# A two-layer attention and expert kernel: its loop of steps replaced by a written-out order for the whole run

## The reference

```
x += attention(ctx, layernorm(x), mask)         # 8 heads of 16, 77 keys, softmax over masked logits
x += ffn(layernorm(x))                          # [x,-x] -> 512 -> 512 -> 128, weights +1/-1 from booleans, relu*2
x += (rmsnorm(layernorm(x)) * g_res) @ W_in.T + b_in + depool(rmsnorm(ctx)[:128], marks)
x += sum of the top 2 of 8 experts, by softmax gate, each with x @ W.T + b
# depool: bidx = cumsum(lens) - 1; boundary_mask.at[bidx].set(1); plug = clip(cumsum(boundary_mask) - 1, 0, 76);
# out row = scan(decay)[plug]; here as a product with pick[k, s] = (plug >= k) * exp(-DT * distance)
```

## Time and profile before

| | us |
|---|---|
| median of 3 runs | 601.62 (600.94 to 605.16) |
| profiled execution, its own time | 600.24 |
| its span | 598.4 |
| TensorE busy / VectorE / ScalarE / POOL | 504.2 / 451.4 / 345.6 / 364.9 |
| mean granted clock of TensorE | 0.958 |
| `a_exponent`, one of its two instructions | 1.105 |
| `rs` of an `rstd` on POOL, L399 | 1.022 |
| `out_x` store, issue to landing | 2.7 |

### The profile page before, as it was taken

The page is one execution under the profiler, slowest core; times in us unless marked ns, Lnnn a source line. Parts: engine busy times, 40 slices in busy tenths (PEclk is TensorE's granted clock), DMA queues, the critical chain, the costliest instruction groups (busy, mean ns, idle before and its releaser), DMA issues.

```text
span 598.4 us, 15067 instructions
## 1 busy us (share of the span) xinstructions
PE 504.2 (84%) x5467; PEld 322.6 (54%) x5467; DVE 451.4 (75%) x1501; ACT 345.6 (58%) x737; POOL 364.9 (61%) x630
## 2 busy tenths in 40 slices
PE   0374298999999999999999999999899999896763
PEld 0263156667565656565665656565757565552320
DVE  4499566888888888888889797979797978865342
ACT  1245267897767676666667676667676666333100
POOL 3103122464858686776868686959595858778457
PEclk9997589999999999999999999999999999999678
DMA  3600001101020202020101101020200000000000
GB/s 77 162 2 1 13 2 46 46 3 46 2 64 1 64 1 63 3 63 2 48 18 35 31 8 57 2 64 2 64 1 25 1 26 2 18 19 1 18 19 18
DMA packets 28578, 16.92 MB, mean 28 GB/s; under 512 B 3828, under 2 KB 28505, under 8 KB 28505
## 3 DMA queue, kind: packets, MB, share of 16 engines
q1 hardware_dynamic: 28504, 15.96, 9.4%
HBM read 11.71 MB, written 4.21 MB: 27 GB/s over the span
## 4 chain that ended last, share of the span: by engine, by line
PE 40%; DVE 22%; POOL 19%; DMA 8%; issue 7%; SPq 2%; ACT 1%; POOLq 0%; DVEq 0%; ACTq 0%
PE pc L1238 14%; DMA cx<-in_ctx 7%; PE pa L1104 5%; PE pb L1140 5%; PE pb L1147 4%; POOL sum L453 4%; DVE st L585 4%; DVE marks L569 3%; POOL rs L399 3%; POOL sum L455 2%; PE pa L1115 2%; PE pb L1159 2%; DVE mx L610 2%; DVE h L690 2%; DVE weighed L780 2%
## 5 line engine op out<-in xcount | busy, mean ns | idle before, releaser
L1238 PE MATMUL pc<-w_moeT,y4T 128*128 128x512 f32 x256 | 129.3, 629 | 12.5 <-DVE weighed L780 7.7
L1147 PE MATMUL pb<-h,w 128*128 128x512 f16 x512 | 121.1, 380 | 0.0
L453 POOL TENSOR_TENSOR sum<-weighed 128x512 f32<-128x512 f32 x64 | 87.3, 1363 | 53.2 <-DVE weighed L780 53.2
L780 DVE TENSOR_TENSOR weighed<-pc,wgt 128x1024 f32<-128x1024 f32 x64 | 78.2, 1221 | 50.2 <-PE pc L1238 47.3
L935 ACT ACTIVATE h<-pb 128x512 f16<-128x512 f32 x128 | 74.3, 595 | 58.5 <-PE pb L1147 30.7
L394 POOL TENSOR_TENSOR ve<-mv,eps 128x4 f32<-128x4 f32 x64 | 18.1, 282 | 133.4 <-DVE mv L592 133.4
L690 DVE SCALAR_TENSOR_TENSOR h<-pb,h 128x512 f16<-128x512 f32 x128 | 84.6, 680 | 11.9 <-ACT h L935 11.9
L898 ACT ACTIVATE prT<-pa,maskT 77x1024 f32<-77x1024 f32 x64 | 67.6, 1105 | 27.7 <-PE pa L1087 27.7
L1238 PEld LDWEIGHTS pc<-w_moeT,y4T 128*128 128x128 f32 x256 | 46.2, 196 | 58.1 <-issue 52.6
L1147 PEld LDWEIGHTS pb<-h,w 128*128 128x128 f16 x512 | 47.8, 98 | 52.7 <-issue 6.7
L399 POOL TENSOR_TENSOR rs<-ve,neg_half 128x4 f32<-128x4 f32 x64 | 65.4, 1022 | 8.9 <-POOL mm L395 0.4
(11 more groups left out here) (159 smaller groups left out, 999.7 us busy)
## 6 DMA issues: line engine op xcount, KB each, us to landing
cx<-in_ctx SPq DMA_DIRECT2D x16, 308.0 KB
xa<-in_x SPq DMA_DIRECT2D x16, 256.0 KB
out_x<-xo SPq DMA_DIRECT2D x16, 256.0 KB, 2.7
plugs<-plug_d SPq DMA_DIRECT2D x16, 77.0 KB
nat<-in_L_ffn_W SPq DMA_DIRECT2D x1, 512.0 KB
k_u<-in_L_ffn_k SPq DMA_DIRECT2D x1, 256.0 KB
k_u<-in_L_ffn_k SPq DMA_DIRECT2D x1, 128.0 KB
mask_b<-mask_b SPq DMA_DIRECT2D x4, 9.6 KB, 2.7
```

The source lines that it names most:

```text
L453: nc.gpsimd.tensor_tensor(sum4[:], both[:, 0:4 * D], both[:, 4 * D:8 * D], ALU.add).then_inc(c_sum4.sem, 1)
L780: nc.vector.tensor_tensor(weighed[:, j % 2, :].rearrange("p (e d) -> p e d", e=E), pc[:].rearrange("p b (e d) -> p (b e) d", d=D), wgt[:, ...
L1147: last = pe.matmul(pb[:, k % 2, :], w2[:, i, c * 128:(c + 1) * 128], h1[:, g.p, part, i, :], start=(i == 0 and part == 0), stop=(i == FC - ...
L1238: last = pe.matmul(pc[:, half, :], y4T[:, g.p, j * S:(j + 1) * S], w_moeT[:, half * 512:(half + 1) * 512], start=True, stop=True)
```

## The change: what it does

- The loop is gone. Each engine's steps are written out for the whole run, and TensorE's steps name the readers of the banks they overwrite (`free`). The steady turn of TensorE has another order than before; the scores of group n + 1 come ahead of the weights of group n.
- The banks are one tensor `ps` of 8. Group 1's attention uses banks 4 to 7, so that it can run beside group 0's. The experts of group 14 alternate between two pairs of banks, those of group 15 use four.
- For groups 14 and 15 VectorE adds the experts of sequences 1 and 3 itself (`e_add`, `e_out` on VectorE, three sums and an add); POOL keeps 0 and 2.
- The marks: the ends are turned on TensorE, split into end // 8 and end % 8, each made one-hot, and 64 products of 77 x 16 by 77 x 8 count them; the counts, cut at 1, go to DRAM and come back in order (`order_counts`), then scan and plug as before.
- `a_distance` moves from VectorE to ScalarE (`far` by Relu, in `a_decays`). The 15 weight loads move to ScalarE's queue. `take_weights` moves to ScalarE. SP loads x and context apart (`load_rows` waits for a_x1 alone), masks first.

```diff
+        def pa(g):
+            return ps[:, 4:8] if g.n == 1 else ps[:, 0:4]
+        def pb(g, k):
+            return ps[:, (0 if g.n == NG - 1 else 4) + k % 2, :]
+        def pm(g, j):
+            b = 6
+            if g.n == NG - 1:
+                b = (2, 6, 0, 4)[j]
+            elif g.n == NG - 2:
+                b = (6, 2)[j % 2]
+            return ps[:, b:b + 2]
+        def on_vector(g, j):
+            return g.n >= NG - 2 and j % 2 == 1
...
+            def load_rows(g):
+                if g.has(4):
+                    sp.wait_ge(a_x1.sem, a_x1.of(g, back=4))
+                sp.dma_start(xa[:, g.f, :].rearrange("s (j d) -> s j d", j=G),
...
+            def order_counts():
+                sp.wait_ge(s_counts.sem, 1)
+                sp.dma_start(mark_d.rearrange("b (a c) -> a b c", c=E), counts[:]).then_inc(plug_out, 16)
+                sp.wait_ge(plug_out, 16)
+                sp.dma_start(marked[:], mark_d).then_inc(marks_in, 16)
...
-                for k in range(lo, hi):
-                    if k >= 2:
-                        dve.wait_ge(made_plug, k - 1)
-                    nc.vector.scalar_tensor_tensor(marks[:, k % 2, :], step[0:B, :], ends[:, k:k + 1], marks[:, k % 2, :],
-                                                   ALU.is_equal, ALU.max).then_inc(made_plug, 1)
...
+                nc.vector.tensor_tensor(eighth[:], ends_f[:, 0, :].unsqueeze(2).to_broadcast([NK, B, S // E]),
+                                        step[:, 0:S // E].unsqueeze(1).to_broadcast([NK, B, S // E]), ALU.is_equal)
+                nc.vector.tensor_tensor(within[:], ends_f[:, 1, :].unsqueeze(2).to_broadcast([NK, B, E]),
+                                        expert[0:NK, :].unsqueeze(1).to_broadcast([NK, B, E]), ALU.is_equal
+                                        ).then_inc(s_ends.sem, 1)
...
+            def count_ends(*readers):
+                free(*readers)
+                pe.wait_ge(s_ends.sem, 1)
+                for b in range(B):
+                    last = pe.matmul(ps[0:S // E, 7, b * E:(b + 1) * E], eighth[:, b, :], within[:, b, :], start=True, stop=True)
+                last.then_inc(p_counts, 1)
```

More of the change, by code:

```diff
@@ L360, in _ @@
+            store(g[14])
+            store(g[15])
             for p in range(2):
@@ new lines, in _ @@
+            b_low(g[0], 6)
+            a_stats(g[5])
+            b_low(g[0], 7)
+            b_low(g[0], 8)
+            b_residual(g[0])
+            c_stats(g[0])
+            b_low(g[1], 0)
+            b_low(g[1], 1)
+            a_weigh(g[2])
+            b_low(g[1], 2)
+            a_residual(g[2])
+            b_stats(g[2])
+            b_low(g[1], 3)
+            b_low(g[1], 4)
+            c_residual(g[0])
+            d_stats(g[0])
+            a_picks(g[2])
+            a_highest(g[4], 0)
@@ new lines, in _ @@
+            b_low(g[2], 3)
+            a_residual(g[3])
+            b_stats(g[3])
+            b_low(g[2], 4)
+            a_picks(g[3])
+            c_residual(g[1])
+            d_stats(g[1])
+            a_highest(g[5], 0)
+            b_low(g[2], 5)
+            a_stats(g[7])
+            e_weigh(g[0], 3)
+            b_low(g[2], 6)
+            a_highest(g[5], 1)
+            a_split_maxima(g[5])
+            b_low(g[2], 7)
+            d_gates(g[1])
+            b_low(g[2], 8)
+            d_top(g[1])
@@ new lines, in _ @@
+            b_low(g[4], 3)
+            a_residual(g[5])
+            b_stats(g[5])
+            b_low(g[4], 4)
+            a_picks(g[5])
+            c_residual(g[3])
+            d_stats(g[3])
+            a_highest(g[7], 0)
+            b_low(g[4], 5)
+            a_stats(g[9])
+            e_weigh(g[2], 3)
+            b_low(g[4], 6)
+            a_highest(g[7], 1)
+            a_split_maxima(g[7])
+            b_low(g[4], 7)
+            d_gates(g[3])
+            b_low(g[4], 8)
+            d_top(g[3])
@@ new lines, in _ @@
+            b_low(g[6], 3)
+            a_residual(g[7])
+            b_stats(g[7])
+            b_low(g[6], 4)
+            a_picks(g[7])
+            c_residual(g[5])
+            d_stats(g[5])
+            a_highest(g[9], 0)
+            b_low(g[6], 5)
+            a_stats(g[11])
+            e_weigh(g[4], 3)
+            b_low(g[6], 6)
+            a_highest(g[9], 1)
+            a_split_maxima(g[9])
+            b_low(g[6], 7)
+            d_gates(g[5])
+            b_low(g[6], 8)
+            d_top(g[5])
@@ new lines, in _ @@
+            b_low(g[8], 3)
+            a_residual(g[9])
+            b_stats(g[9])
+            b_low(g[8], 4)
+            a_picks(g[9])
+            c_residual(g[7])
+            d_stats(g[7])
+            a_highest(g[11], 0)
+            b_low(g[8], 5)
+            a_stats(g[13])
+            e_weigh(g[6], 3)
+            b_low(g[8], 6)
+            a_highest(g[11], 1)
+            a_split_maxima(g[11])
+            b_low(g[8], 7)
+            d_gates(g[7])
+            b_low(g[8], 8)
+            d_top(g[7])
@@ L988, in _ @@
         @block.tensor
         def _(pe):
[L991 to L1000 removed]
+            pe.wait_ge(made_pool, 2)
```

1963 lines of the change are left out of this document (1485 added, 478 removed).

## The result

The median after is **566.06 us** (564.72 to 567.37, 4 runs), beside 602.23 for the kernel before on the same chip (600.94 to 605.16, 4 runs): ratio 0.939, 95% interval 0.935 to 0.944. The forecast was 553 with a range of 541 to 568, so the time lies in the range, but outside the 545 to 558 of the forecast itself. The profiled execution has a span of 564.1 us and a time of 565.91. The sum of the prediction, made against spans, said 551: it promised 47.5 us, and 34.3 came.

What follows compares the result with a forecast made beforehand. The middle was taken as bound by TensorE's own work, 31.3 us a group nearly a floor; gains at head, fill, middle and drain, -10.5 -7 -3 -11 +2 -18 = -47.5 from span 598.4, gave span 551, time 553; range 541 to 568.

Steps and rivals of the forecast that it cites:

- rival A: Head later: slower products, weights landing behind context loads, exponents at half clock; first layer 66 to 68; +8 us; chance 0.14.
- B: Middle keeps its loss, as thin covers fail and another wait replaces that for x; +11 us, 564; chance 0.12.
- Part 1: Head, marks: 77 VectorE steps of 0.27 us removed; 64 TensorE products added, 4 us, ending near 16 us, costing 1.
- Two more trips through DRAM: Head: counts out and marks in precede make_plug, now ahead of a_highest(g[0],0); first maximum near 26 to 28 us, before 23.3.
- Part 2: Head: ScalarE issues the 15 weight loads, 7.1 us; group 1's x goes out 13 us sooner; weights in at 15 to 18.
- Part 3: Head and fill, two attentions side by side: group 0's first layer at 60 us (58 to 64), before 70.57; gain 10.5.
- wrong would be: Signs that would refute the forecast: a middle above 31, a first layer after 66, or a drain over 50 us.
- Part 4: Middle: x loaded behind a_x1 alone, so its 1.63 us wait goes; 30.0 us a group from 31.3; 11 us better.
- The cover of expert 0's weighing: Middle: gate product through weighing takes 6.2 us, TensorE work in between 7.1; it holds with 0.9 over.
- Part 5: Drain, from the last b_last's end: 39.5 us (36 to 46), before 63.1; 18 better after 5.4 moved ahead; 2 given back.
- 7 of work ahead: By group 0's first layer TensorE has also done later groups' weights, values, turns and scores: 7 us of work ahead.
- 3 of fill: Fill to the steady state: before, 5.6 us idle and about 5 by lower clock; now 4.5 and 3 lost; 3 better.

Runs made afterwards that it cites:

- few marks: The kernel before with 8 of the 77 steps of marks, the other marks left out; median 596.01 us, ratio 0.988.
- loads held: The kernel after, but SP waits for all 15 weight loads before loading group 2 and later; median 560.73 us, ratio 0.927 to the kernel before.
- x apart: The kernel before with x loaded behind a_x1 alone, each load with its own semaphore, order of steps untouched; median 586.68 us, ratio 0.971.

## Why the prediction was right and where not

The sign and the range were right, the head was wrong, the middle was right in kind and its gain too high by 3 us, and the drain was right in its sum. The range held because it had room for rivals A and B: A came, and a part of B. Of the signs named beforehand, the first layer (71.6, near 60 forecast), the first maximum (34.5, 26 to 28) and the middle's start-to-start (30.42, 29.8 to 30.2) missed; no wait for zT over 6 us, no DMA wait before the statistics and the drain held.

**Part 1, the marks: right in both ends.** The 64 products took 1.75 us, start to end, 0.03 each; I took 4, between 1 and 8.2. They ended at 13.3 us and not near 16. The steps' 11.59 us are real (few marks: first layer at 59.0). "Two more trips through DRAM" I had in the order of work but not with their place: the counts are taken behind the wait for the weights (26.86), 13 us after the products had them ready. It cost nothing in the kernel after, where the marks were back when VectorE came to them; with loads held it waited 2.8 us for them.

**Part 2 failed: "I take the weights to be in at 15 to 18 us".** They were in at 23.7. I had read that the transfers are the limit, and gave them their old landing less the issue time; but with SP freed, the loads of groups 2 and 3 start at 8.6 to 10.7 us and share the 16 engines with the weights (share 0.85 to 1.17 from 4 to 18 us), and the scattered load is last in the queue. Earlier issue of work that is not urgent delayed the work that is. The two runs that took each away show the landing at 18.4 and 19.9; the gain in time is shown for the first of them alone. With the 10.8 us of VectorE's own work behind it, the landing is the whole delay of the first maximum.

**Part 3: the walk was right on its order and short on its length.** From first maximum to first layer I gave 33 us and it took 37.2: group 0's values came faster than walked (15.4 us against 18), but from there on 21.7 against 15, because TensorE has 18.7 us of work there at a clock of 0.66. Of that, 1.8 are the clock (19.9 at 1.00); but even there TensorE is busy 15.8 us, more than the whole stretch that I walked. With the 7.5 us of the first maximum (34.5 against 27) this is the whole miss of 11.6. It is rival A's event, at 71.6 beyond its 66 to 68, by two of its three mechanisms: mainly the landing behind context loads, and with 1.8 us the low clock. The list of "wrong would be" named it: a first layer after 66.

**Part 4: right cause, size off.** The split of the loads is the gain, shown alone; no DMA wait is left in front of x's statistics. I took 30.0 us a group and it is 30.42: 3.3 us over eight groups. The cover of expert 0's weighing held (0.4 us of wait in six groups). What I missed is that TensorE is busy 0.4 us more a group in this order than in that of before with x apart, for the same products (their ends are modelled, and no run isolates a cause).

**Part 5: right, 39.6 for 39.5.** It was right in its sum; that it is right to 0.1 is luck, as the same steps took up to 42.1. Of its reasons the banks are the one over-weighed: I ascribed to them the fall from 3.36 to 1.23 a turn, and they give 3.2 to 3.6 us; what is left to the order is three quarters.

Together: 11.6 for the head and 3.3 for the middle, less 1.7 for all the rest, are the 13.2 us by which the sum missed. That 1.7 is small because two large misses cancel. From the first layer to group 5's values it took 2.9 us more than before where 10 less were forecast (7 of work ahead and 3 of fill); from group 13's values to the last b_last it took 7.4 less (99.6 against 107.0) where 6.6 more were forecast (5.4 of work moved there from the drain and 2 given back, less 0.8). One reason is where a group's values stand in the new turn: by those of group 5 TensorE has done some 85 more of its products, besides the 64 for the marks. So these cuts cannot tell whether the 7 and the 3 came as such. TensorE's idle time in the fill fell from 5.6 to 3.2 us and its clock rose from 0.96 to 0.98, which fits the 3.

## What to carry to other kernels

When a strict order puts the consumption of a shared load ahead of the first useful work, ask what else the freed queue will now start: issuing group loads earlier made the weights, on which everything waited, later. Hold back what is not urgent (5.3 us on the landing here), issue the small scattered load first (3.8 us on the landing, its worth in time not shown), and move set-up work into an engine's later idle stretch, but only behind what the next engine waits for: the same move was worth nothing with a few steps misplaced and 1.7% with them right. And before crediting a new order with a gain, run the one dependency that changed alone: here the split of one load gave the whole gain of the middle.

## What the runs showed of the hardware that was not expected

- The granted clock fell to 0.90 and 0.92 in two middle turns with TensorE 95% busy or more (34.3 us for a turn of 31.3 in the kernel with few marks; 34.6 for one of 31.4 in the one with the weights on ScalarE's queue, 392.0 to 426.6 us). The same turns of the kernel before ran at 1.00. Just ahead of each fall (at 319.5 and 392.3 us) TensorE had sat idle for zT, 1.79 and 1.72 us, where the kernel before waits 0.8. The third row is from the kernel before: an idle stretch of 1.99 us with no fall behind it. So such a stretch alone doesn't decide it, and the cause is open.

```profile
319.15 1.52 PE L1140 MATMUL pb<-zT,w 128*128 128x512 f16 x4 [1.79 <-DVE zT L687]
```
```profile
391.08 1.02 PE L1140 MATMUL pb<-zT,w 128*128 128x512 f16 x4 [1.72 <-DVE zT L672]
```
```profile
510.13 1.96 PE L1159 MATMUL pb<-w,h 128*128 128x128 f16 x32 [1.99 <-DVE h L690]
```

- A load of 4 KB in single elements took 11 us from issue to landing behind the others (12.04 to 23.69), and was what the first user waited for; issued first, it was no longer the last.
- The product hitw, 0.224 to 0.966 us before, took 0.224 to 0.226 in all 16 groups after, and POOL's sum at most 1.283 us against 1.717: the two did not run into each other in the middle, which the new order of VectorE and POOL may explain; no run isolates it.
